# One change to a four-stage kernel: a packed triangular inverse, decayed rows made inside the recurrence, and a reordered seam between heads

## The reference, cut to what matters

```python
mixed = hidden_states @ W_qkv
z = (hidden_states @ W_z).reshape(B, T, NV, DV)
beta = sigmoid(hidden_states @ W_b)
g = -exp(A_log) * softplus(hidden_states @ W_a + dt_bias)
conv = sum(xp[:, i:i + T, :] * conv_w[:, i] for i in range(4))   # xp: mixed, 3 zero rows ahead
q, k, v = split(silu(conv))                                      # 16, 16 and 32 heads of 128
q, k = l2norm(q) * 128 ** -0.5, l2norm(k)
for t in range(T):                                               # per value head
    S = S * exp(g[t])
    S = S + beta[t] * k[t][:, None] * (v[t] - k[t] @ S)[None, :]
    o[t] = q[t] @ S
o = o * rsqrt(mean(o * o) + 1e-6) * norm_w * silu(z)
out = o @ W_out
```

## Time and profile before

| | us |
|---|---|
| median of three runs | 2123.1 (2117.54 to 2123.35) |
| the profiled execution's own time | 2117.7 |
| its span, first to last instruction | 2115.8 |
| PE busy | 1917.6 (91%) |
| DVE busy | 1505.7 (71%) |
| ACT busy | 984.2 (47%) |
| POOL busy | 759.0 (36%) |
| one pass of the head loop (1402.03 to 1488.86) | 86.83 |

### The profile page before, as it was taken

How to read it: one execution, slowest core, us unless ns; L and a number is a source line. 1 busy time by engine, 2 the same in 40 slices (tenths; PEclk the granted TensorE clock), 3 DMA queues, 4 the chain that set the end, 5 groups by cost and what they waited for, 6 DMA issues and landing times.

```text
span 2115.8 us, 43478 instructions
## 1 busy us (share of the span) xinstructions
PE 1917.6 (91%) x15082; PEld 1402.3 (66%) x15082; DVE 1505.7 (71%) x2430; ACT 984.2 (47%) x2535; POOL 759.0 (36%) x685
## 2 busy tenths in 40 slices
PE   4578886888799999999999999999999999999998
PEld 3246662333555687877878778787687777877877
DVE  5786771111677687787787877878778787787887
ACT  1012224777213354645545455455564555645544
POOL 4730002110300334616336164362543624526343
PEclk9689998999899999999999999999999999999999
DMA  6635661000122200010010000100001001010010
GB/s 245 209 91 200 184 178 55 26 20 1 55 60 70 82 17 35 5 35 30 15 35 10 30 30 15 35 30 10 30 15 35 30 10 40 5 35 30 15 45 20
DMA packets 75254, 111.75 MB, mean 53 GB/s; under 512 B 23318, under 2 KB 56742, under 8 KB 72006
## 3 DMA queue, kind: packets, MB, share of 16 engines
q1 hardware_dynamic: 71694, 102.32, 15.1%
q0 software_dynamic: 3072, 8.39, 1.3%
q10 hardware_dynamic: 446, 0.48, 0.1%
HBM read 85.80 MB, written 28.52 MB: 54 GB/s over the span
## 4 chain that ended last, share of the span: by engine, by line
PE 51%; DVE 16%; issue 4%; ACT 3%; POOL 0%; DVEq 0%; ACTq 0%; POOLq 0%
PE ps L1273 5%; PE ps L1311 4%; PE ps L1321 4%; DVE conv L1862 3%; DVE P L2034 3%; DVE P_term L2031 3%; PE ps L1544 3%; PE ps L1493 3%; PE ps L1533 3%; PE ps L1428 3%; PE ps L1417 3%; PE ps L1546 3%; PE ps L1520 2%; PE ps L1450 2%; PE ps L1525 2%
## 5 line engine op out<-in xcount | busy, mean ns | idle before, releaser
L1862 DVE SCALAR_TENSOR_TENSOR conv<-raw,tap_st,conv 128x1024 f32<-128x1024 f32 x204 | 299.5, 1468 | 3.6
L1273 PE MATMUL ps<-xnT,w_conv_st 128*128 128x512 f32 x544 | 247.6, 599 | 0.0
L1842 POOL TENSOR_TENSOR o<-o,silu_z 128x256 f32<-128x256 f32 x128 | 138.5, 1082 | 255.5 <-DVE silu_z L1882 141.7
L816 DVE TENSOR_REDUCE m_part<-ps 128x1 f32<-128x640 f32 (+7 forms) x176 | 176.4, 1027 | 67.1 <-PE ps L667 53.5
L1726 POOL TENSOR_TENSOR gmask_Q<-upto,g 128x2048 f32<-128x2048 f32 x17 | 61.4, 3611 | 363.5 <-PE ps L1500 335.5
L998 ACT ACTIVATE probs<-ps 128x1024 f32<-128x1024 f32 (+7 forms) x256 | 145.9, 660 | 58.1 <-PE ps L933 28.7
L1273 PEld LDWEIGHTS ps<-xnT,w_conv_st 128*128 128x128 f32 x544 | 98.9, 191 | 101.1 <-issue 96.2
L1565 ACT COPY raw<-ps 128x512 f32<-128x512 f32 x136 | 80.7, 594 | 173.4 <-PE ps L1273 173.4
L1822 POOL TENSOR_TENSOR kq_decayed<-conv,decay_rows 128x1024 f32<-128x1024 f32 x64 | 159.3, 2521 | 0.0
L1321 PE MATMUL ps<-w_z_st,xnT 128*128 128x256 f32 x512 | 148.8, 393 | 0.0
L903 POOL DMA_INDIRECT slot_outputs<-scratch_slots_y,token_slots x32 | 30.6, 958 | 310.9 <-POOLq L496 202.0
(11 more groups left out here) (345 smaller groups left out, 4728.9 us busy)
## 6 DMA issues: line engine op xcount, KB each, us to landing
decay_rows<-scratch_egc SPq DMA_DIRECT2D x17, 1024.0 KB, 4.7
w_conv_st<-in_w_conv SPq DMA_DIRECT2D x17, 512.0 KB, 3.3
scratch_slots_x<-yacc SPq DMA_DIRECT2D x8, 1024.0 KB, 14.9
slot_rows<-scratch_slots_x SPq DMA_DIRECT2D x16, 512.0 KB, 4.7
scratch_slots_y<-slot_outputs SPq DMA_DIRECT2D x16, 512.0 KB, 3.4
w_gate_up<-in_gu SPq DMA_DIRECT2D x8, 768.0 KB
w_gate_up<-in_gu SPq DMA_DIRECT2D x32, 192.0 KB
kq_decayed<-in_gu SPq DMA_DIRECT2D x22, 256.0 KB, 2.8
```

Source lines behind the costliest of these rows:

```text
L816: dve.tensor_reduce(dst, src, AX.X, ALU.max).then_inc(s_max, 1)
L1273: mm = pe.matmul(ps[:, 6 + n % 2, :], wc[:, k, (n // 2) * P:(n // 2 + 1) * P], m.xnT[:, k, (n % 2) * HALF:(n % 2 + 1) * HALF], start=k == ...
L1842: g.tensor_tensor(oc, oc, zs[:, c, :], ALU.mult).then_inc(s_oz, 1)
L1862: op = dve.scalar_tensor_tensor(out=cv[:, t, :], in0=raw[:, t, at:at + T], scalar=tap[:, t, at:at + 1], in1=cv[:, t, :], op0=ALU.mult, op1 ...
```

## The change

What it does, part by part:

- Packed inverse. Within the doubling levels only the diagonal 64x64 halves of P and Q are nonzero, so both are now stored packed, [128, chunk, 64] in place of [128, chunk, 128]: `pd` and `qd`, the two halves of the old `gm_q` buffer. The spreads (L2104 on DVE, one on POOL) write 128x512 in place of 128x1024. A transpose takes two chunks at once, so there are 4 per value head in place of 8. Its result holds the halves of odd and even chunks crossed over, and ACT sorts them with four copies of 64x256 (`halves`), or, after the first level, leaves them crossed (`pd[:, e]` copied as it is) and lets the next products find them by `place`. The products X = U Q and Q X have 32 moving columns in place of 64. In the second level `place` puts a product's operands or results in the other half of rows or columns for half of the chunks. `base` gives X and Q X banks of their own per level.
- Projections. Of the eight projections of the next head, 4 (was 5) stand ahead of the transposes of the spread, one behind each of the two, one in each of the two levels.
- The seam. Transposes of the first half of the outputs now stand between the `kk` products, the second half behind two output products; `project_out` goes 2 and 2 in place of 3 and 1. On DVE the three last `conv_op`s of v's second head stand at the start of the next pass, ahead of and behind the `ua` products; `gate_outputs(i, 1)` stands behind the `ua` products; three of four `add_out` stand behind `uc`. `uc` is a reduction of `u32`, ACT writes U's diagonal blocks into PSUM (bank 5), and ACT starts `pc`.
- Decayed rows. `kqe` of head `i + 1` is made by POOL inside the recurrence of head `i`, for one chunk at a time: `decayed(c)`, two operations of 128x256 once PE has done with chunk c of the old rows. Those of the first head are made ahead of the loop. The decay rows' DMA moves to the start of the pass.
- `gmask(i + 1)` also waits for the k convolution of head `i + 1` (`s_cvd`, i * 4 + 6).
- Room: the expert stage ahead of the loop uses `e_p` and `ke` as scratch in place of `kqe`; the residual input is loaded into `row` in place of `egr`; masks of five unused levels are gone.

The diff, cut to its core:

```diff
+        xs32 = xs[:, :, 0:NC // 2, :].rearrange("p e c (q n) -> p e (c q) n", q=2)
+        gm_room = gm_q[:].rearrange("p e c n -> p (e c n)")
+        qd = gm_room[:, 0:NC * P].rearrange("p (e c n) -> p e c n", e=2, c=NC)
+        pd = gm_room[:, NC * P:].rearrange("p (e c n) -> p e c n", e=2, c=NC)
...
+        def place(lv, c, h):
+            j, hi = c // 2, int(h is HI)
+            if lv == FIRST:
+                return h, c, 0, c, 0, c
+            return (LO, HI)[c % 2], 2 * j + hi, hi, j, c % 2, j
+
+        def halves(e):
+            turned = ps[:, 2 + e, :].rearrange("p (j h n) -> p j h n", h=2, n=64)
+            return [(h, odd, turned[(LO, HI)[odd], :, int(h is HI), :]) for h in (HI, LO) for odd in range(2)]
+
+        def base(lv, e):
+            return (e, (4, 0)[e], (4, 1)[e])[lv - FIRST]
...
             with sp.Fori(0, NK) as i:
+                sp.wait_ge(s_kqe, i * 7 + 7)
+                decay_rows(m.egc_rows[bass.ds(2 * i + 2, 2), :])
                 sp.wait_ge(s_pj, i * 8 + 8)
...
                 for b in range(4):
+                    if b == 2:
+                        pe.wait_ge(s_e, i * 4 + 4)
+                        for n in range(2):
+                            turn_outputs(i, n)
...
-                                mm = pe.matmul(dst, ua[h, e, c, 1, h], gm_q[h, e, c, :].rearrange("p (b t s) -> p b t s", t=2, s=s)[:, :, 0, :],
+                                g, at, bank, slot, _, _ = place(lv, c, h)
+                                dst = ps[g, bank + base(lv, e), slot * 32:(slot + 1) * 32].rearrange("p (b s) -> p b s", s=s)
+                                mm = pe.matmul(dst, ua[h, e, c, 1, h], qd[h, e, c, :].rearrange("p (b t s) -> p b t s", t=2, s=s)[:, :, 0, :],
                                                start=True, stop=True)
...
-                                mm = pe.matmul(ps[h, e, c * 64:(c + 1) * 64], e_p[h, e, c, h], xs[h, e, c, :], start=True, stop=True)
+                                g, at, _, _, bank, slot = place(lv, c, h)
+                                mm = pe.matmul(ps[h, bank + base(lv, e), slot * 32:(slot + 1) * 32], pd[g, e, at, :], xs32[g, e, at, :], start=True, stop=True)
...
-                    if lv == FIRST:
-                        project(i + 1, 7)
+                    project(i + 1, 6 + lv - FIRST)
...
-                    nc.scalar.copy(chunks(e_p[:, e]), two_banks(2 + 2 * e)).then_inc(s_pt, 1)
+                    if lv == FIRST:
+                        nc.scalar.copy(chunks(pd[:, e]), ps[:, 2 + e, :]).then_inc(s_pt, 1)
+                    else:
+                        for h, odd, src in halves(e):
+                            last = nc.scalar.copy(e_p[h, e, odd::2, h], src)
+                        last.then_inc(s_pt, 1)
+                tanh_conv(i + 1, 1)
...
+            def decayed(c):
+                at = slice(c * P, (c + 1) * P)
+                for e in range(2):
+                    op = g.tensor_tensor(kqe[:, e, :, at], cv[:, 0:2, at], egr[:, e, at].unsqueeze(1).broadcast_to([P, 2, P]), ALU.mult)
+                op.then_inc(s_kqe, 1)
...
-                for e in range(2):
-                    for a in range(2):
-                        g.tensor_tensor(kqe[:, e, a, :], cv[:, a, :], egr[:, e, :], ALU.mult).then_inc(s_kqe, 1)
...
                 pool.wait_ge(s_x, i * ND + ND)
+                pool.wait_ge(s_cvd, i * 4 + 6)
                 gmask(i + 1)
...
+                for c in range(1, NC):
+                    if c < NC - 1:
+                        pool.wait_ge(s_su, i * 14 + 2 * c + 1)
+                    else:
+                        pool.wait_ge(s_aw, i * NC + NC)
+                    passed()
+                    decayed(c)
...
+                    gate_z(c - 1)
+                    if c == 4:
+                        rsqrt_outputs(i, 0)
+                gate_z(NC - 1)
+                rsqrt_outputs(i, 1)
...
             with dve.Fori(0, NK) as i:
-                gate_outputs(i, 1)
+                for k in range(2, TAPS):
+                    conv_op(i, 3, k)
...
+                gate_outputs(i, 1)
+                conv_op(i, 3, TAPS)
+                add_out(i, 0)
...
-                dve.tensor_tensor(uc[:], u32[:, :, 0, :], u32[:, :, 1, :], ALU.add).then_inc(s_uc, 1)
-                add_out(i, 3)
+                dve.tensor_reduce(uc[:], u32[:].rearrange("p u t i -> p u i t"), AX.X, ALU.add).then_inc(s_uc, 1)
+                for n in range(1, 4):
+                    add_out(i, n)
```

More of the change, by code:

```diff
@@ L1452, in _ @@
                 pe.wait_ge(s_u32, i * 5 + 5)
+                pe.wait_ge(s_um, i + 1)
+                pe.wait_ge(s_cvd, i * 4 + 4)
                 turn_v(1, 4)
                 pe.wait_ge(s_vn, i * 16 + 8)
-                for n in range(5):
+                for n in range(4):
                     project(i + 1, n)
```

185 lines of the change are left out of this document (97 added, 88 removed).

## The result

| | before | changed |
|---|---|---|
| median, us (4 runs each, lowest to highest) | 2123.22 (2117.54 to 2124.14) | 2054.69 (2052.01 to 2055.58) |
| ratio, 95% interval | | 0.9682 (0.9667 to 0.9697) |
| profiled execution, its span | 2117.7, 2115.8 | 2055.6, 2053.4 |
| pass 8 of the head loop | 86.83 | 82.06 |
| predicted | | 2090 (2040 to 2132) |

The changed kernel is 68.5 us faster, where 27 were forecast from the profiled execution and 33 against the median. The time is inside the range. A pass lost 4.77 us in place of 1.7. (Pass 8 is counted from 0 here, so it is the ninth; the pass that was read before is the ninth too.)

The account below looks back on a forecast made before the run. PE's list of work was taken to set each head-loop pass; the terms summed to -1.7 us a pass, x 16 = -27, from 2117.7 to 2090 us, with an 8-in-10 range of 2040 to 2132.

Parts of the forecast that it names:

- Transposes: Spread and levels: 24 fewer transposes per pass at 0.115 us each, 2.76 us less.
- Halved columns: X and the product behind it, both levels: half the moving columns save only 0.3 us a pass, ends 0 and 4.2.
- Where the second level's products sit: Second level: X costs 0, the product behind it +1.0 us a pass because its neighbours share rows.
- The seam: Ahead of the block-row products: the 0.95 us PE gap goes; delayed gate_outputs costs +0.2, ends 0 and +1.5.
- The levels' gaps: PE gaps at the masks of the two levels: -0.1 us at the first, -0.5 at the second.
- Gates at the first chunk: First state product: gmask holds up the DVE tap ahead of the state copy, +1.5 us, ends 0 and +2.3.
- Decayed rows in the recurrence: Recurrence: decayed(c) on POOL can hold up DVE's tap, +0.2 us a pass, ends 0 and +2.1.
- packing pays more: Rival: second level at 32 ns and gmask meets no tap, -4.2 us a pass, 2050 us; chance 0.21.
- Columns count: Rival: the products halve with their moving columns, -5.6 us a pass, 2028 us; chance 0.08.
- one after the other: Rival: both second-level products run at 63 ns a record, +1.3 us a pass, 2138 us; chance 0.13.
- PE waits: Rival: saved PE work returns as waits for masks, copies and taps, 0 a pass, 2118 us; chance 0.16.
- X's records at 16 ns: Sign against the forecast: X's records halving to 16 ns, where 30 to 32 ns was expected in the first level.

Follow-up runs that it names:

- one half at a time: Second-level products reordered, all of the low half first, then all of the high, against the changed kernel: one run 2030.78 us, pass 82.60.
- split last level: Each last-level product made as two of 32 moving columns, against the changed kernel: one run 2109.91 us (before 2120.90 there), pass 85.26.
- Runs of four products in one quarter: Second-level products reordered so four in a row use one quarter, against the changed kernel: one run 2071.39 us, pass 8 84.14.

## Why the prediction was right or wrong

**What bounds it: right.** PE's list of work sets the pass before and after; of the 4.77 us, 5.24 are PE work gone and 0.47 idle time added.

**Transposes: right.** 2.76 forecast. L1492 takes 0.49 and 0.44 us up to the next start, L1525 0.97 twice, 2.87 in all against 48 x 0.115 = 5.52: 2.65 less.

**Halved columns: right that they are worth next to nothing; the size came by luck.** 0.3 forecast for all groups. The first level did lose 0.30 (3.96 us, against 6.41 from 1440.38 to 1446.79 less a projection of 1.82 and the gap of 0.33), but the columns are not the cause: with 64 columns in their place it still takes 3.99, and the pass is 0.06 longer. What gave the other 0.27 is open. The page TensorE: Matmul & The Clock Gate of the Trainium skill, "LDWEIGHTS (loading the stationary operand)", ties the load's time to the stationary columns alone; the kernel with 64 columns agrees in that 32 or 64 moving columns make no difference.

**Where the second level's products sit: the step that failed.** I put +1.0 us, ends 0 and +2.0. Before, the two groups took 4.26 us: from 1448.63 to 1453.54, less the gap of 0.65, where 1453.54 is the start of what came behind them:

```profile
1453.54 1.97 PE L1493 MATMUL ps<-ident,gmask_Q 128*128 128x128 f32 x16
```

Now they take 2.20 (1416.07 to 1418.44, less 0.17). Measured: -2.06, which is 3.06 us a pass or 49 us over 16 passes away from the term and outside its ends. Of the -2.06, 1.8 come from the quarters, as the kernel with two of them shows. The error was to treat 32 ns as the best pace. The rows had one quarter at 63 ns and two at 32, half of it, and the step from these to four quarters at 16 was open; I reasoned only from whether neighbours share rows, and gave the term no end below nothing. The two rules of the Trainium skill that I set against each other can now be told apart in this kernel: TensorEngine Tiling (Array Packing), "Key Properties", with different tiles loading and multiplying in parallel, agrees; TensorE: Matmul & The Clock Gate, "The mechanism", with overlapping loads only where the row group differs, would leave X with its rows kept (the kernel with one half at a time) near the 60 ns of one quarter, and the run got 22 to 24. There the measurement decides.

**The seam: right in its gap, small in its worth.** The gap ahead of the block-row products went as forecast (-0.95), and `gate_outputs` cost nothing (+0.2 forecast). But before is not the right measure for either part: with the new inverse, the decayed products left at the seam would cost 2.4 us or more a pass, since they reach into the chain of the small inverse, and the old order of the seam 3.25, of which 1.33 is the clock. These parts keep the rest of the gain; I priced them against the old pass alone. The seam also became shorter by something for which the forecast has no term: the transposes and products of the outputs, now in two parts each, take 8.73 us from start to start in place of 9.12. Why is open.

**The levels' gaps: nearly.** Forecast -0.1 and -0.5. The 0.33 at the first mask became 0.30 and 0.21 ahead of the transposes and X (+0.18), the 0.65 became 0.17 (-0.48).

**Gates at the first chunk: right.** +1.5 forecast, ends 0 and +2.3; the wait went from 0.17 to 1.93, +1.76, by the tap of 4.51 us beside a `gmask` of 3.61 as described. Moving the tap gave 1.60 back. The Trainium skill's GPSIMD Engine Reference, "Key points", has VectorE and GpSimd contend where the vector operation has two SBUF inputs. The runs agree: the tap with its two SBUF inputs was held up, the copies that read PSUM were not.

**Decayed rows in the recurrence: right, at nothing.** +0.2 forecast; a chunk takes 3.65 us as before, and the two operations (1.42 us) fall where DVE reads PSUM.

**The sum.** -2.65 - 0.30 - 2.06 - 0.95 - 0.30 + 1.76 = -4.50 a pass. The outputs' transposes and products add -0.39, the block-row products -0.11 (4.01 us from 4.12, which began with a wait), and small lengthenings elsewhere +0.25, among them 0.14 behind the last level's second group (L1540). That is -4.75 of the 4.77. Sixteen such passes would be 76 us; the profiled execution's span became 62.4 shorter. The first pass lost only 1.14 (85.26 to 84.12), the pass with the low clock 3.48, the last pass with all behind it 2.75, and the loop began at 716.0 us in place of 708.9. Of these 7.1 us, 1.6 lie in one expert's turn, where PE waits 1.29 us for the DMA of its weights and the 1 MB of decay rows is now loaded too (that the one causes the other is not shown); 5.6 were there already ahead of the experts, with the granted clock lower in that execution. Whether any of the 5.6 belongs to the change was not tried.

**Rivals.** The first, that packing pays more, came nearest (2050), but by luck: it had 32 ns in the second level and no block by `gmask`. In truth the block came and the pace was 17, and the two misses, +1.76 and about -2, nearly cancel. *Columns count*, *one after the other* and *PE waits* are refuted by the kernel with 64 columns, by the 17 ns, and by the 5.24 us of PE work that became 4.77 of time. I had written that X's records at 16 ns would prove the forecast wrong; in the second level they do (17).

## What to carry to other kernels

With small products, count how many quarters of the array neighbours in the order use, not their moving columns: 64 records took 3.84 us in one, 1.98 in two and 1.07 in four, and an extra transpose to spread them was repaid twice. When an operation of POOL must run near the critical path, place it beside DVE operations that read PSUM, and take taps and additions on SBUF out of its way. And price each part of a change inside the new schedule as well as the old: two parts that looked worth under 1 us were worth 2.4 and 3.3 inside the new pass.

## What the hardware showed that was not expected

- Four quarters in turn: 17 ns a 64x64 f32 record, the same with 32 and with 64 moving columns. In one quarter: 60 ns with 32 columns (split last level), 63 with 64.
- Runs of four products in one quarter: about 35 ns, little over half of what one quarter takes. Why is open.
- The granted clock fell in steady passes that were changed little: 0.56 over 3.88 us behind a 1.93 us wait in the old seam order, 0.75 over 6.9 us behind 7.7 us of one-quarter products with PE busy throughout. The first cost 1.33 us a pass. Of the first 15 passes, the clock fell behind the same 1.93 us wait in 1 in the changed kernel, in 4 with one half at a time, in 14 with runs of four products (32 columns), and in all with the old seam order. In the two kernels with the tap moved, which don't have the wait, it fell in none. Why it falls in some passes only is open.
- A small DVE addition of about 0.4 us took 2.00 when it met one of POOL's four products (11.46 us together), and a tap of 1.28 took 4.51 beside a `gmask` of 3.61: the loss goes by the operation of the other engine and can be several times the length of the one held up.
